# Layer 0's edge weights as sixteen 32x32 matmuls into four banks, the four block products in one piece, and the logits spread ahead of the projection

## The reference

```
msg_s = (s_n @ Ws_src)[src] + (s_n @ Ws_dst)[dst]           # msg_v alike
y0, y1 = rsh[:, 0], rsh[:, 1:4]
w1 = rbf @ W_rbf                                            # 16 -> 224 edge weights
m1_s, m1_v = _cg_tp(msg_s, msg_v, y0, y1, w1[...])          # w * s * y0, w * (v . y1), w * s * y1, w * v * y0, w * (v x y1)
a = sum(leaky(m1_s @ W_alpha) * alpha_dot)                  # 4 heads
amax = segment_max(a, dst); ex = exp(a - amax[dst]); alpha = ex / segment_sum(ex, dst)[dst]
val_s, val_v = m1_s @ Ws_val, m1_v @ Wv_val                 # gated by sigmoids
h = (second tensor product of val with y) @ Ws_vlin, Wv_vlin
agg = segment_sum(alpha * h, dst)
```

## Time and profile before

| | |
|---|---|
| median of 3 runs | 10095.94 us (10092.63 to 10127.31) |
| span of the profiled execution | 8679.9 us, in which PE is busy 88%, DVE 84%, POOL 69%, ACT 37% |
| mean granted clock of TensorE over the span | 0.947 of full speed |
| own time of the profiled execution | not recorded beside its span; the median of the runs is 1416 us longer than the span |
| layer 0's loop | from about 355 to 6074 us of the span |
| TENSOR_TENSOR to `blocks` (L1030) | 782 + 782 of 681 and 683 ns, 501.0 + 502.1 us |
| MATMUL for the edge weights (L767) | 3128 records, 884.8 us |

### The profile page before, as it was taken

How to read it: one execution, slowest core, us unless ns; L and a number is a source line. 1 busy time by engine, 2 the same in 40 slices (tenths; PEclk the granted TensorE clock), 3 DMA queues, 4 the chain that set the end, 5 groups by cost and what they waited for, 6 DMA issues and landing times. The chain is left out here.

```text
span 8679.9 us, 218293 instructions
## 1 busy us (share of the span) xinstructions
PE 7627.6 (88%) x60373; PEld 5771.5 (66%) x60374; DVE 7274.4 (84%) x17597; ACT 3252.4 (37%) x8375; POOL 6016.9 (69%) x5890
## 2 busy tenths in 40 slices
PE   2599999999999999999999999887968888888888
PEld 1487777877877787877787778776644444444445
DVE  4699999999999999999999999775368888888886
ACT  1244444444444444444444444332222222222223
POOL 0477777777777777777777777651037777777774
PEclk9799999999999999999999999987569999999999
DMA  4344444444444444444444444321012222222222
GB/s 53 78 101 99 102 100 101 102 100 101 101 102 101 101 101 99 102 100 100 100 101 102 101 102 100 77 75 29 11 37 67 67 67 67 67 67 67 67 67 61
DMA packets 616622, 725.52 MB, mean 84 GB/s; under 512 B 284132, under 2 KB 390884, under 8 KB 616573
## 3 DMA queue, kind: packets, MB, share of 16 engines
q0 software_dynamic: 225408, 385.00, 20.4%
q1 hardware_dynamic: 391165, 339.92, 15.3%
HBM read 708.40 MB, written 16.06 MB: 83 GB/s over the span
## 5 line engine op out<-in xcount | busy, mean ns | idle before, releaser
L778 PE MATMUL bank_pair<-w_msg,blocks 128*128 128x160 f32 (+2 forms) x15640 | 2078.7, 288 | 126.8 <-DVE blocks L1030 98.2
L720 POOL DMA_INDIRECT got_src<-src_tab,idx x1564 | 1661.5, 1062 | 659.4 <-POOL idx L714 358.5
L778 PEld LDWEIGHTS bank_pair<-w_msg,blocks 128*128 128x128 f32 x15640 | 1972.7, 192 | 218.5 <-DVE blocks L1030 218.5
L1504 POOL DMA_INDIRECT gotf<-f_tab,idx x1568 | 1702.3, 1086 | 514.2 <-issue 477.4
L720 POOL DMA_INDIRECT got_dst<-dst_tab,idx x1564 | 1486.3, 950 | 528.7 <-issue 503.7
L802 PEld LDWEIGHTS bank_pair<-weights_t,product 128*128 128x128 f32 x12896 | 1498.7, 195 | 309.9 <-issue 295.6
L802 PE MATMUL bank_pair<-weights_t,product 128*128 128x128 f32 x12896 | 1575.5, 281 | 9.5 <-ACT weights_t L932 8.2
L1545 PE MATMUL bank_pair<-val,to_node 128*128 128x385 f32 x3136 | 1247.6, 545 | 5.0 <-DVE val L1659 5.0
L1600 ACT ACTIVATE val<-pre,y_edge 128x160 f32<-128x160 f32 x1568 | 542.8, 417 | 1534.0 <-DVE pre L1640 1531.4
L1545 PEld LDWEIGHTS bank_pair<-val,to_node 128*128 128x128 f32 x3136 | 621.6, 208 | 536.8 <-issue 270.1
L767 PE MATMUL bank_pair<-edge,w_edge 64*128 64x512 f32 x3128 | 884.8, 642 | 9.5 <-DVE blocks L1030 9.5
(11 more groups left out here) (268 smaller groups left out, 11950.3 us busy)
## 6 DMA issues: line engine op xcount, KB each, us to landing
rbf<-in_rbf SPq DMA_DIRECT2D x391, 256.0 KB
dst_bc<-in_dst_rows SPq DMA_DIRECT2D x391, 256.0 KB
y<-in_y SPq DMA_DIRECT2D x391, 128.0 KB
y<-in_y SPq DMA_DIRECT2D x391, 96.0 KB
gotf<-f_tab,idx POOLq DMA_INDIRECT x1568, 2.7
got_src<-src_tab,idx POOLq DMA_INDIRECT x1564
got_dst<-dst_tab,idx POOLq DMA_INDIRECT x1564
rbf<-in_rbf SPq DMA_DIRECT2D x392, 32.0 KB, 1.7
```

Of the source, the lines that this page charges most:

```text
L720: pool.indirect_dma_start(out=buf[slot][:, t, :], out_offset=None, in_=table[:, :], in_offset=bass.IndirectOffsetOnAxis(ap=idx[slot][:, c: ...
L778: return nc.tensor.matmul(to, blocks[rows, k, P * t:P * t + P], w_msg[rows, c0:c1], start=start, stop=stop)
L1504: pool.indirect_dma_start(out=got[k][:, t, :], out_offset=None, in_=f_tab[:, :], in_offset=bass.IndirectOffsetOnAxis(ap=idx[k][:, t:t + 1] ...
```

## The change

The eight bands of `edge` are put in another order (the input `y7` has the harmonics 0, 1, 0, 2 for the first 64 rows, a constant one for rows 64 to 80, and 2, 3, 1 for the last 48), so that each of the sixteen 32x32 pieces of the weights finds its two bands in one strip of 32 rows. `EDGE_TILES` gives for each block and each strip of 32 output rows the strip of input rows and the band. Each of the sixteen cells of the array is used once. The four blocks have a bank each; the two new ones lie where `scalars` lie, so PE now waits for `tanh` and `leaky` of the group before ahead of the edge weights, and no longer ahead of the message stage.

```
+ONE = -1
+EDGE_SLOTS = ((0, 1), (0, 2), (ONE, 2), (3, 1))
+EDGE_TILES = (((0, 0), (0, 1), (1, 2), (3, 3)),
+              ((2, ONE), (2, 2), (3, 3), (0, 1)),
+              ((1, 0), (1, 0), (0, 0), (1, 0)),
+              ((3, 3), (3, 1), (2, 2), (2, ONE)))
-        ebank = [psum[1][:, 512 * b:512 * b + 512] for b in range(2)]
+        ebank = [psum[1 + b // 2][:, 512 * (b % 2):512 * (b % 2) + 512] for b in range(4)]
...
-                def weigh(pair, half):
-                    r = slice(64 * half, 64 * half + 64)
-                    nc.tensor.matmul(ebank[half], w_edge[r, pair, :], weigh.operand[r, :], start=True,
-                                     stop=True).then_inc(s["weighed"], 1)
+                def weigh_edges(slot):
+                    for b in range(4):
+                        for j in range(4):
+                            r = slice(32 * EDGE_TILES[b][j][0], 32 * EDGE_TILES[b][j][0] + 32)
+                            c = slice(32 * j, 32 * j + 32)
+                            last = nc.tensor.matmul(ebank[b][c, :], w_edge[r, b, c], edge[slot][r, :], start=True, stop=True)
+                        last.then_inc(s["weighed"], 1)
...
                     if now:
-                        pe.wait_ge(s["scaled"], g + 1)
                         if mid:
                             pe.wait_ge(s["block_done"], g * 4)
-                        weigh(0, 0)
-                        weigh(0, 1)
+                            pe.wait_ge(s["tanh"], g)
+                            pe.wait_ge(s["leaky"], g)
+                        wait_apart(pe, s["scaled"], g + 1, s["tick_p"])
+                        weigh_edges(slot)
...
-                    if now:
-                        pe.wait_ge(s["block_done"], g * 4 + 2)
-                        weigh(1, 0)
-                        weigh(1, 1)
+                    if mid:
+                        pe.wait_ge(s["turned_copied"], turned)
+                        pe.wait_ge(s["logit_wide"], g)
+                        spread_logits(other).then_inc(s["logit_turned"], 1)
...
+                                if mid:
+                                    spread_logits(other).then_inc(s["more_back"], 1)
                                 wait_apart(pe, s["more_scaled"], w + 1, s["tick_p"])
...
+                            if respread:
+                                wait_apart(dve, s["more_back"], w + 1, s["tick_v"])
...
-                def messages(g, first):
-                    for k in (first, first + 1):
+                def messages(g):
+                    for k in range(4):
...
-        "y6": y.reshape(NG_PAD, GE, 4).transpose(0, 2, 1)[:, [0, 1, 2, 3, 1, 2], :],
+        "y7": y.reshape(NG_PAD, GE, 4).transpose(0, 2, 1)[:, [0, 1, 0, 2, 2, 3, 1], :],
```

More of the change, by code:

```diff
@@ L175, in _, with put_edge @@
                 o_ss, o_sv, o_vs, o_vv0, o_vv1 = 0, CS, 2 * CS, 2 * CS + CV, 2 * CS + 2 * CV
[L177 to L183, removed]
-                for j in range(3):
[L185 to L190, removed]
+                def put_edge(block, col, frm):
+                    row, harmonic = EDGE_TILES[block][col]
+                    first = 32 * row + NB * EDGE_SLOTS[row].index(harmonic)
+                    put(w_edge[first:first + NB, block, 32 * col:32 * col + 32], frm)
+                put_edge(0, 0, Wr[:, o_ss:o_ss + 32])
+                put_edge(1, 0, Wr[:, o_sv:o_sv + 32])
+                put_edge(2, 3, Wr[:, o_ss + 32:o_ss + 64])
+                put_edge(3, 3, Wr[:, o_sv + 32:o_sv + 64])
+                for j in range(3):
+                    put_edge(0, j + 1, Wr[:, o_vv0:o_vv0 + 32])
+                    put_edge(1, j + 1, Wr[:, o_vv1:o_vv1 + 32])
+                    put_edge(2, j, Wr[:, o_vs:o_vs + 32])
+                    put_edge(3, j, Wr[:, o_vv1:o_vv1 + 32])
                 Wa, Ws, Wv = A["W_alpha"], A["Ws_val"], A["Wv_val"]
@@ L521, in layer0 @@
         "weights_turned", "weights_copied", "window_sum", "win_scaled", "merged", "more_far", "more_spread", "more_top", "more_step", "more_shifted", "more_weights", "more_factors",
-        "more_turned", "more_copied", "more_sum", "more_held", "more_projected", "more_scaled", "more_added", "more_rescale", "zeroed", "step", "span", "meta")}
+        "more_turned", "more_copied", "more_sum", "more_held", "more_projected", "more_scaled", "more_added", "more_back", "more_rescale", "zeroed", "step", "span", "meta")}
     s.update(K["ticks"])
@@ L672, in load_edge @@
                     rows = group_of(A["rbf"], g)
-                    y = group_of(A["y6"], g)
+                    y = group_of(A["y7"], g)
                     sp.dma_start(rbf8[slot][:], rows.unsqueeze(0).broadcast_to([8, NB, GE])).then_inc(s[f"edge{slot}"], 16)
                     sp.dma_start(y8[slot][0:64, :], y[0:4, :].unsqueeze(1).broadcast_to([4, NB, GE])).then_inc(s[f"edge{slot}"], 16)
-                    sp.dma_start(y8[slot][80:128, :], y[1:4, :].unsqueeze(1).broadcast_to([3, NB, GE])).then_inc(s[f"edge{slot}"], 16)
+                    sp.dma_start(y8[slot][80:128, :], y[4:7, :].unsqueeze(1).broadcast_to([3, NB, GE])).then_inc(s[f"edge{slot}"], 16)
                 def load_dst(g, slot):
@@ L866, in step @@
                         last.then_inc(s["message_s"], 1)
+                        if mid:
+                            pe.wait_ge(s["vector"], g * 2)
                         for t in range(3):
@@ L1029, in messages @@
                         dve.wait_ge(s["weighed"], g * 4 + k + 1)
-                        dve.tensor_tensor(blocks[:, k, :], ebank[k % 2], (turned_low, turned_high)[k // 2][:],
+                        dve.tensor_tensor(blocks[:, k, :], ebank[k], (turned_low, turned_high)[k // 2][:],
                                           ALU.mult).then_inc(s["block_done"], 1)
```

19 lines of the change are left out of this document (4 added, 15 removed).

## The result

The kernel after takes 11251.66 us (median of 4 runs, 11234.03 to 11282.38), the kernel before 10095.06 us beside it (10092.63 to 10127.31). The ratio is 1.114, with a 95% interval of 1.111 to 1.117: 1157 us slower, far outside the range of 9925 to 10210 us.

What follows compares the result with a forecast made beforehand. POOL's round in layer 0, 14.08 us a group, was taken to bound the kernel. From 10095.9 us, -25 (late groups), -5 (first groups) and +3 (repeated spread) gave about 10070 us, range 9925 to 10210.

Steps and rivals of the forecast that it cites:

- 1416 us lie around the span: Whole run: the profile's span of 8679.9 us against the runs' 10095.94 leaves 1416 us outside it, kept unchanged.
- in the steady groups POOL's round is untouched: 0: Layer 0's steady groups: POOL's round stays near 14.1 us, so the change gains and costs 0 there.
- POOL sets the pace: Layer 0: POOL waits for nobody, 14.08 us a group; PE's nearly equal round is not the pace, DVE having 0.65 us slack.
- Part 1: PE's edge weights: sixteen matmuls take 1.3 us instead of 2.1, so PE gains 0.8 us a group.
- Rival B: PE's edge weights: the sixteen don't run side by side, taking 2.6 us (about 10215 us in all) or 4.2 (+730); chance 0.10.
- Part 2: New waits for `tanh` and `leaky` ahead of PE's edge weights: price 0, since DVE wants the first block 2.6 us later.
- Part 3: DVE's four block products in one piece: price 0, up to +0.2 us; for the third block DVE waits for PE no more.
- Part 4: Spread ahead of projection: PE's round about 13.05 us, 0.75 to spare; `near` no longer waits for the spread.
- `sums` stretched under POOL's add: DVE's accumulation into `sums` would still be stretched to the end of POOL's add, a sign that the forecast is right.
- Part 6: Loads: same sizes and three DMAs a group, 0.8 MB more input of some 28; taken as 0, with +35 us as an end.
- C: Rival, POOL's gathers: the last gather ahead of the add is stretched in every second group, +110 us, about 10180; chance 0.11.

Runs made afterwards that it cites:

- before, first profile: The unchanged kernel before, in the profile the prediction was read from: a span of 8679.9 us, while its runs' median was 10095.94 us.
- before again: The kernel before, unchanged, profiled once more: 10094.41 us; the profiled run took 10107.63 us with a span of 10105.8 us.
- order_only: The kernel after's order, banks and waits, but four 64x128 block matmuls instead of the sixteen 32x32: 9770.39 us, 0.968 of the kernel before; repeated, 0.971.
- eight 64x64: The order of the kernel after, with the four block products made by eight 64x64 matmuls: 10063.29 us, 0.994 of the kernel before.
- few rows: The kernel after with every gather after the first two groups fetching 32 rows instead of 128: 11676.84 us, 1.155 of the kernel before.
- the twelve one-column matmuls: order_only with twelve one-column matmuls ahead of its four block products, which overwrite their results: 10493.81 us, 1.039 of the kernel before.

## Why the prediction was wrong

**The step that failed** is the one under "the change, part by part": "1416 us lie around the span, where no row shows anything", and with it "in the steady groups POOL's round is untouched: 0". A profile 14% shorter than every timed run is not a profile with 1416 us around it. It showed an execution in which PE's signals are on time. The timed runs are of another kind, in which the round is 16.4 us and PE's late signals are in it. In that kind the change costs 19.2 - 16.4 = 2.8 us a group, 2.8 x 391 = 1100 us of the 1157. By POOL's rows these are 3.8 us more of waiting (5.15 for 1.39), less 1.0 of shorter gathers (7.99 for 9.02), and 0.1 more in the index copy. Behind layer 0 nothing changed (3230 us for 3234).

The term that the sum put at nothing is what the sixteen matmuls do to the row behind them. This table has it, for 2000 to 4000 us; "late" is the time from the end of the sum's last matmul to its recorded signal, and both middle columns are medians.

| kernel | ratio | POOL's round, us | sum of products, us | late, us | clock |
|---|---|---|---|---|---|
| before, first profile | | 14.1 | 3.84 | 0.01 | 1.00 |
| before again | 1 | 16.4 | 3.84 | 1.9 | 0.94 |
| order_only | 0.968 | 15.5 | 3.84 | 0.8 | 0.99 |
| eight 64x64 | 0.994 | 16.4 | 3.84 | 0.7 | 0.97 |
| after | 1.114 | 19.2 | 6.2 | 0.01 | 0.90 |
| after, no loads | 1.028 | 17.1 | 5.6 | 0.01 | 0.95 |
| after, half the gathers | 0.965 | 15.4 | 4.2 | 0.01 | 0.97 |
| after, no gathers | 0.921 | 14.3 | 3.84 | 0.01 | 1.00 |
| before, no transfers | 0.965 | 15.4 | 3.84 | 0.01 | 0.95 |

The lower clock is a small part: PE's busy time a group, in which it shows, is 14.3 us in the kernel before again and 14.9 in the kernel after, 0.6 of the 2.8 us at most.

Point by point:

- *POOL sets the pace.* True in the earlier trace rows, not in the timed runs of either kernel: in the kernel after POOL waits 436.4 us of 2000 for PE.
- *Part 1, sixteen matmuls in 1.3 us.* 1.08 us. Rival B, that they don't run side by side, is refuted. The Trainium skill, TensorE: Matmul & The Clock Gate, "Part 3: Packing small matmuls — row/col tiling", had given an estimate of 1.6 us; the measurement is below it. The strict order of starts and ends by the same page is there in the records, but each record lasts 0.6 us and the next starts 7 to 11 ns after it, so it did not hold them up.
- *Part 2, new waits at 0.* Order_only has them and is 3% faster, so they are cheap. Not tried apart.
- *Part 3, "for the third block DVE waits for PE no more".* It waits 2.28 us, for a signal whose matmuls were long done. In order_only that wait is gone, and POOL's add waits 2.3 us in 2000 where it waited 126.5 in the kernel before. But its edge product waits 131.9 us where it waited 42.4, so the two together fall only from 1.39 to 1.04 us a group. The larger part of the 0.9 us that order_only gains a group is shorter gathers, 8.3 us for 9.0; why they are shorter was not tested.
- *Part 4, the spread.* Priced at 0 in the steady groups; alone it gains 1.1%.
- *`sums` stretched under POOL's add.* No longer: in the kernel after one takes 258 ns in the median and 300 at most (L1003, 1000 to 5000 us).
- *Part 6, the price if the inputs were the 1416 us.* 0.8 of 28 MB of 1416 us is 40, not 35; it carries nothing here.
- *The rivals.* None names this mechanism. B and C had the sign, with about a tenth of the size at their likelier prices (145 and 110 us).

**What is shown and what is not.** Shown: the loss needs both the short matmuls in the new place and the gathers; it goes with the number of gathers and not with their rows; it appears as late signals of PE and as gaps in PE's rows that end on nothing. Loads add to it (1.114 to 1.028 without them). Not shown: which path they share, and whether it is the issuing of a gather, its descriptors or its signals that counts. One more thing in the traces bears on it. I counted the recorded semaphore updates of each group between 2000 and 4000 us. The first profile of before has 236 a group, among them 4.0 of `weighed`, as the program makes them. The kernel before again has 157 a group and 3.3 of `weighed`, order_only 151, the kernel after 167: in these stalled runs about a third of the updates have no record. Without gathers `weighed` is complete again (4.0 of 115 a group). Each gather raises its semaphore by 16, with 32 rows too, so the program counts 128 for its eight (124 on record in the first profile); the five loads leave 50 updates on record a group in the run without gathers. One reading is that updates and records of PE and of the DMA engines queue at one place. It fits few rows (same count, no gain), half the gathers (64 fewer, most of the loss gone) and no loads (50 fewer, some of it gone). Two things speak against it: the first profile has more updates on record in less time (236 in 14.1 us) and no stall, and without loads `weighed` is nearly complete (3.98) and the round is still 17.1 us. So it stays a guess.

The Trainium skill, NOTIFIC — the notification-queue block, "7.1 Overflow: three behaviours, one of which stalls the engine", says that the block's inner pipeline holds back its producers rather than lose a record, so that recording can throttle an engine. Stalls that come with missing records agree in the first half and not in the second, since here records are also lost. No run here is without recording, so whether the loss belongs to the program or to its recording stays open. It is in every timed run of the kernel after.

## What to carry to other kernels

Hold the span of a profile against the times of the runs before anything is read from it; when they differ by 14%, the profile shows another kind of execution, and its waits are not those that are timed. A row of many short matmuls is not priced by its columns alone: where many small transfers land, each with its signals, try it with fewer and wider matmuls, and with fewer transfers. Change order and form apart: here the order gained 3% of the time before, and the form then cost 15% of it.

## What the hardware showed unexpectedly

- Sixteen fp32 matmuls 32x32x512, each of two passes, took 1.08 us together, hardly more than two 64x128x512 (1.05).
- PE's signals can reach all waiting engines at one moment, 2 to 3 us after the matmuls: 3012.28, 3012.32, 3012.47 for work that ended at 3009.37 and 3010.43.
- A gather of 32 rows takes POOL 0.87 us (L726, got_dst, median with few rows) where one of 128 takes 0.95 (kernel after), so a quarter of the rows saves 0.08 us.
- After 1.9 us in which PE waited, the granted clock of its next stage was 0.71 in the mean (kernel before without transfers; 4.45 us became 6.12). Over whole runs it is 0.864 in the kernel after, 0.877 in the kernel before and 0.918 without gathers, but it doesn't simply follow the time: with the twelve one-column matmuls, 4% slower than before, it is 0.907.
